# Second attention on one Trainium2 core: explicit job tables, the last maxima turned one batch on, and two small bank reads moved from VectorE to ScalarE

## What is computed

```python
mixed_q, mixed_k, mixed_v = h @ wq + bq, h @ wk + bk, h @ wv + bv
glo = jnp.mean(mixed_q, axis=1, keepdims=True)
c = jnp.tanh(mixed_q @ wfq + bfq + (glo @ wfg + bfg))
p, z = jnp.sum(heads(c) * up, -1), jnp.sum(heads(c) * uz, -1)
P, Z = sigmoid(p) * S, sigmoid(z) * S
G = -(j - P[..., None]) ** 2 * 2.0 / Z[..., None] ** 2
probs = softmax(q @ k.T / sqrt(8) + G)
x = layernorm(h + (probs @ v) @ wo + bo)
```

## Time and profile before

| what | value |
|---|---|
| median of 3 runs | 1585.86 us (1583.54 to 1586.01) |
| the profiled execution | 1584.24 us |
| its span | 1582.5 us |
| mean granted clock of PE | 0.966 |
| PE busy | 1426.4 us, 90% of the span |
| DVE busy | 1126.6 us, 71% |
| ACT busy | 989.4 us, 63% |
| POOL busy | 832.0 us, 53% |

### The profile page before, as it was taken

The page is one execution under the profiler, slowest core; times in us unless marked ns, Lnnn a source line. Parts: engine busy times, 40 slices in busy tenths (PEclk is TensorE's granted clock), DMA queues, the critical chain, the costliest instruction groups (busy, mean ns, idle before and its releaser), DMA issues. The chain is left out here.

```text
span 1582.5 us, 37924 instructions
## 1 busy us (share of the span) xinstructions
PE 1426.4 (90%) x12249; PEld 809.1 (51%) x12249; DVE 1126.6 (71%) x2583; ACT 989.4 (63%) x2120; POOL 832.0 (53%) x1008
## 2 busy tenths in 40 slices
PE   5999999999999999999979999888888888887837
PEld 4666666666666666666646776522332332332225
DVE  5657666666767657666677888878888888888733
ACT  2656656656666666666647888647677677665711
POOL 4766776776776776776665545511231231232533
PEclk9999999999999999999979999979999999999969
DMA  6100000100000000000000000241111111111000
GB/s 193 30 22 23 27 21 20 27 20 20 27 20 20 27 20 20 25 22 20 21 17 1 0 0 21 60 116 49 34 33 50 30 37 47 30 45 31 14 24 17
DMA packets 71099, 50.82 MB, mean 32 GB/s; under 512 B 30875, under 2 KB 59408, under 8 KB 70896
## 3 DMA queue, kind: packets, MB, share of 16 engines
q1 hardware_dynamic: 67936, 45.70, 10.6%
q10 hardware_dynamic: 1760, 3.02, 0.6%
q0 software_dynamic: 1344, 1.33, 0.3%
HBM read 38.18 MB, written 13.28 MB: 33 GB/s over the span
## 5 line engine op out<-in xcount | busy, mean ns | idle before, releaser
L620 ACT ACTIVATE prob<-score_ps,nmax 128x512 f32<-128x512 f32 (+3 forms) x512 | 266.8, 528 | 148.6 <-DVE nmax L691 148.6
L691 DVE TENSOR_REDUCE nmax<-score_ps 128x1 f32<-128x512 f32 (+3 forms) x512 | 224.9, 480 | 184.9 <-PE score_ps L498 180.0
L1974 DVE TENSOR_REDUCE a_nm<-a_s 128x1 f16<-128x512 f32 x512 | 323.7, 685 | 44.3 <-PE a_s L1810 41.6
L1932 ACT ACTIVATE a_pt<-a_st 128x1024 f32<-128x1024 f32 x256 | 261.8, 1024 | 120.8 <-PE a_st L1814 119.7
L1810 PE MATMUL a_s<-a_kop,a_qop 64*128 64x512 f16 x512 | 184.4, 403 | 61.9 <-DVE a_nm L1974 54.7
L510 PE MATMUL pt_ps<-ident,prob 128*128 128x128 f32 x1280 | 182.7, 273 | 2.6 <-ACT pt L629 1.4
L629 ACT ACTIVATE pt<-pt_ps 128x512 f32<-128x512 f32 (+1 forms) x192 | 102.9, 536 | 123.8 <-PE pt_ps L510 123.8
L1814 PE MATMUL a_st<-a_qop,a_kop 64*128 64x512 f16 x512 | 175.0, 394 | 0.0
L1846 PE MATMUL a_pv<-a_pt,a_vaug 128*32 128x256 f32 x2048 | 167.3, 399 | 7.6 <-ACT a_pvs L1937 6.1
L814 POOL TENSOR_SCALAR_AFFINE_SELECT k_h<-k 64x512 f16<-64x512 f32 x130 | 81.0, 623 | 169.9 <-ACT k L653 157.4
L510 PEld LDWEIGHTS pt_ps<-ident,prob 128*128 128x128 f32 x1280 | 145.6, 141 | 35.2 <-ACT pt L629 1.6
(11 more groups left out here) (386 smaller groups left out, 3130.8 us busy)
## 6 DMA issues: line engine op xcount, KB each, us to landing
r_bc<-r_parts SPq DMA_DIRECT2D x128, 128.0 KB, 2.8
a_qop<-q_parts SPq DMA_DIRECT2D x64, 64.0 KB, 1.9
a_kop<-k_parts SPq DMA_DIRECT2D x64, 64.0 KB, 1.9
x_tok<-in_L_attn_input_dram SPq DMA_DIRECT2D x4, 512.0 KB, 12.8
r_parts<-rsum SPq DMA_DIRECT2D x128, 2.0 KB, 2.1
q_parts<-a_q_h SPq DMA_DIRECT2D x16, 128.0 KB, 2.3
k_parts<-a_k_h SPq DMA_DIRECT2D x16, 128.0 KB, 2.3
e_w<-in_L_ffn_w_dram SPq DMA_DIRECT2D x1, 2048.0 KB, 9.6
```

Of the source, the lines that this page charges most:

```text
L620: ins = nc.scalar.activation(prob[h][:, P_OFF[c]:P_OFF[c] + w], score_ps[u][:, col:col + w], ACT.Exp, bias=nmax[h][:, c:c + 1], accum_out= ...
L691: ins = nc.vector.tensor_reduce(nmax[h][:, c:c + 1], score_ps[u][:, col:col + P * (c + 1)], AX.X, ALU.max, negate=True)
L1932: nc.scalar.activation(pt[kc % 2][r][:, :, :], st_ps[r][:, :, :], ACT.Exp, scale=1.0 / SC).then_inc(exp_done[r], 1)
L1974: nc.vector.tensor_reduce(nm[g % 2][:, c, hh:hh + 1], s_ps[j][:, :], AX.X, ALU.max, negate=True).then_inc(max_done[j], 1)
```

## The change

The two tables become one table for each kind of batch, by half slot. In a middle batch the same twenty jobs run. nm3 moves from half slot 31 to half slot 0 of the next batch, ctx1 from 1 to 30 of the batch before; behind every job with a part on DVE stands a half slot without a job. GB comes before K. The bank reads of V and of GB move from DVE to ACT. In the prelude K and GB change places.

```diff
-        AHEAD = {1: "XT", 2: "Q", 3: "K", 4: "GB", 5: "F", 6: "PZ", 11: "CF", 12: "V"}
+        AHEAD = {1: "XT", 2: "Q", 3: "GB", 4: "K", 5: "F", 6: "PZ", 11: "CF", 12: "V"}
...
-PREP = ["XT", "Q", "K", "GB", "F", "PZ", "CF", "V"]
-MIDDLE = {4: "nm0", 8: "nm1", 9: "CT", 10: "OUT", 12: "nm2", 13: "RX", 15: "RD"}
-END = {0: "ctx1", 1: "XT", 2: "Q", 3: "RC", 4: "ctx2", 5: "K", 6: "GB", 7: "F", 8: "ctx3", 9: "PZ", 11: "CF", 12: "ctx0",
-       13: "V", 14: "RL", 15: "nm3"}
+PREP = ["XT", "Q", "GB", "K", "F", "PZ", "CF", "V"]
+JOBS = {
+    "first": {1: "XT", 3: "Q", 4: "GB", 5: "K", 8: "nm0", 9: "F", 11: "PZ", 16: "nm1", 21: "CF", 22: "ctx0", 24: "nm2", 29: "V",
+              30: "ctx1"},
+    "middle": {0: "nm3", 1: "XT", 3: "Q", 4: "GB", 5: "K", 6: "ctx2", 8: "nm0", 9: "F", 11: "PZ", 14: "ctx3", 16: "nm1", 17: "CT",
+               19: "OUT", 21: "CF", 22: "ctx0", 24: "nm2", 25: "RX", 27: "RL", 29: "V", 30: "ctx1"},
+    "last": {0: "nm3", 5: "RC", 6: "ctx2", 8: "nm0", 14: "ctx3", 16: "nm1", 17: "CT", 19: "OUT", 22: "ctx0", 24: "nm2", 25: "RX",
+             27: "RL", 30: "ctx1"},
+    "tail": {0: "nm3", 6: "ctx2", 7: "RC", 14: "ctx3", 16: "CT", 18: "OUT", 26: "RX", 29: "RL", 30: "RD"},
+}
...
-BEHIND = ["ctx1", "ctx2", "ctx3", "CT", "OUT", "RX", "RL"]
-PARTS_OF = {"first": ("ahead", "own"), "middle": ("ahead", "own", "behind"), "last": ("own", "behind", "RC"),
-            "tail": ("behind", "RC", "RD")}
+BEHIND = ["nm3", "ctx2", "ctx3", "CT", "OUT", "RX", "RL"]
...
 def uses(kind):
-    order = [t[at] for at in range(SLOTS) for t in (MIDDLE, END) if at in t]
-    return [u for u in order if part_of(u) in PARTS_OF[kind]]
+    return [JOBS[kind][h] for h in sorted(JOBS[kind])]
...
     def act_steps(act):
...
+        def gate_bias(kind, b, nb):
+            used(kind, b, "GB")
+            nc.scalar.activation(gbias[:, :], misc[:, 0:1], ACT.Identity, bias=bf[:, :], scale=1.0 / S).then_inc(misc_out, 1)
+
+        def values(kind, b, nb):
+            act.wait_ge(vaug_done, G * nb)
+            used(kind, b, "V")
+            nc.scalar.activation(v32[:, :], misc[:, :], ACT.Copy).then_inc(misc_out, 1)
...
     def dve_steps(dve):
...
-        def values(kind, b, nb):
-            dve.wait_ge(vaug_done, G * nb)
-            used(kind, b, "V")
-            nc.vector.tensor_copy(v32[:, :], misc[:, :]).then_inc(misc_out, 1)
-
-        def gate_bias(kind, b, nb):
-            used(kind, b, "GB")
-            nc.vector.scalar_tensor_tensor(gbias[:, :], misc[:, 0:1], 1.0 / S, bf[:, :], ALU.mult, ALU.add).then_inc(misc_out, 1)
...
-                    for half, table in ((0, MIDDLE), (1, END)):
+                    for half in range(2):
...
-                        if at in table:
-                            shared_use(table[at], kind, b)
+                        job = JOBS[kind].get(2 * at + half)
+                        if job:
+                            shared_use(job, kind, b)
...
-            def maxima_t(kind, b, _, g):
+            def maxima_t(kind, b, cb, g):
                 for k in range(2):
-                    pe.wait_ge(max_done[k], 32 * b + 8 * g + 8)
+                    pe.wait_ge(max_done[k], 32 * cb + 8 * g + 8)
...
-            def maxima(kind, b, _, g):
+            def maxima(kind, b, cb, g):
 
-                act.wait_ge(nm_in[(g + 2) % G], NM_LOADS * (b + 1) if g >= 2 else NM_LOADS * b)
+                act.wait_ge(nm_in[(g + 2) % G], NM_LOADS * (cb + 1) if g >= 2 else NM_LOADS * cb)
```

More of the change, by code:

```diff
@@ L1513, in coefficients @@
             nc.scalar.activation(coef_t[:, :], misc16[:, 0:S], ACT.Copy).then_inc(misc_out, 1)
-        return used, high, {"XT": high("XT", xt_h, xt_hi), "Q": queries, "K": keys, "F": gates, "PZ": sigmoids,
-                            "CF": coefficients}
+        return used, high, {"XT": high("XT", xt_h, xt_hi), "Q": queries, "K": keys, "GB": gate_bias, "F": gates, "PZ": sigmoids,
+                            "CF": coefficients, "V": values}
     def dve_steps(dve):
@@ L1545, in centres @@
             nc.vector.tensor_scalar(cent[:, :, :], cent[:, :, :], S / 32.0, -(S - 1) / 64, ALU.mult, ALU.add).then_inc(cent_done, 1)
-        return used, low, {"XT": low("XT", xt_h, xt_l, xt_hi), "V": values, "GB": gate_bias, "PZ": centres}
+        return used, low, {"XT": low("XT", xt_h, xt_l, xt_hi), "PZ": centres}
     def pool_steps_(pool):
@@ L1718, in shared_use @@
             def shared_use(name, kind, b):
[L1719 to L1725, removed]
+                batch = {"ahead": b + 1, "behind": b - 1}.get(part_of(name), b)
+                if name[-1] in "0123":
+                    step(name[:-1], kind, b, batch, int(name[-1]))
+                else:
+                    step(name, kind, b, batch)
             def batch(kind, b):
```

## The result

The changed kernel takes 1594.11 us (median of 4 runs, 1592.94 to 1594.53), the kernel before beside it 1585.34: a ratio of 1.0056, 95% interval 1.0038 to 1.0073. Five further runs later gave 1593.30 against 1586.27, 1.0043 [1.0029, 1.0057]. So the change costs 7 to 9 us. The profiled execution took 1593.99 us with a span of 1592.3, which is 9.8 more than before.

The account below looks back on a forecast made before the run. No engine is full, so waits between engines bound the kernel. Middle batches +12.2, first batch -.7 and last batch -.5 give +11 us on the profiled 1584.24, 1595.2, and with the runs' median 1596 us; range 1580 to 1603.

Parts of the forecast that it names:

- main case: Whole kernel: jobs standing alone show their whole latency, so the change is slower, 1592 to 1598 us; chance .50.
- Spreading and its savings in the middle batches: Six middle batches: new half slots sum to 59.77 against 57.7 us, 2.0 more each, 12.2 in all.
- the rules' 57.7: Old middle batch followed half by half with timing rules read from the timelines: 57.7 us against the measured 58.0.
- bound from below: Middle batch: at in-a-row costs, CT, PZ, OUT and RX give back .3 + .9 + .8 + .5; some 57.3 us.
- nm3: Halves 31 and 0: moved one batch on, they take 2.97 instead of 3.76 us, a gain of .8.
- The reads on ACT: V and gate bias halves: DVE's .60 and .31 us leave its path, covered by slack between ACT's exponentials.
- The clock: Rival: all six middle batches run at a mean clock of 0.97, +3.2 us, 1599; chance .15.
- The first batch: First batch: gains on V and a hidden Q, loses on ctx1, gives away nm3; -.7 us.
- The last batch: Last batch: ctx2's transposes under RC gain 2.4 us, ctx3, CT, RX and ctx1 alone cost 1.9; -.5.
- Tail and prelude: Tail: nm3 later but T of half 0 sooner, 0 within 1 us; prelude: 0 within .5.
- no more alone: Rival: jobs cost no more alone, DVE waits before PZ, OUT, CT, RX stay, only savings remain: 1572 us; chance .20.
- The rival of a late row of nm3: Rival: nm3's row is late for half 4, PE waits .5 to 1 us per batch, up to 1602; chance .05.

Follow-up runs that it names:

- e1: The kernel before, with PZ moved from half slot 19 to 20 and OUT from 20 to 22: 1601.38 us, ratio 1.0104.
- e3: The kernel before, with V's and the gate bias's bank reads moved from DVE to ACT and nothing else: 1582.69 us, ratio .9983.
- e4: The changed kernel with another table, keeping ctx3, CT, PZ, OUT, V in a row at half slots 17 to 21: 1558.71 us, .9831 against the kernel before.
- e12: The table of e4, with the shift, exponentials and choice of the seventh batch's routing one slot later in the tail: 1556.28 us, .9809 against the kernel before.

## Why the prediction was right, and which steps were wrong

The forecast was 1596.0 and the time 1594.1, slower by .56%, inside the main case's 1592 to 1598. The mechanism is shown: the same DVE waits appear where they were put, one pair of moved jobs in the old kernel costs 1.73 a batch, and putting one job back takes it away. That the total is 1.2 us from the 1595.2 worked out for the profiled execution is luck in part. Against the sum, the middle batches cost 1.1 more (two errors that cancel: 4.3 less from the places, 5.5 more from the clock), the last batch 2.3 more, the first 2.5 less, and the start and what follows the last batch 2.1 less.

- *Spreading and its savings in the middle batches* were put at 12.2 us (2.0 a batch) and measured 7.9 (1.31 at full clock). By quarters the new table came out at 14.2, 14.6, 16.8 and 13.8 against 14.3, 14.7, 17.0 and 13.8, so the new side was good to .4. PZ measured 3.42 (3.44), OUT 3.85 (3.90), CT 2.68 (2.65), XT 2.61 (2.65), RX 3.04 (2.96), V 2.23 (2.25). The transposed maxima took 1.66, not 1.77, three times in a batch. The other .3 came from the base: the new table's sum was set against the rules' 57.7 instead of the measured 58.02, although the text knew of the gap. In its bound from below, CT's .3 does not follow from its own halves either, 2.65 against 2.50.
- *Inside that sum*, nm3 was put at .8 a batch. In the old table it gave 1.1 to 1.2, since ctx1 behind it also got quicker; in the new one, where ctx1 stands elsewhere, halves 31 and 0 take 1.20 + 1.66 instead of 3.76, so .9. The reads on ACT were put at .9 (.60 and .31). They gave .45 in the old table, all of it V's, and .1 in the new one; that step failed: the gate bias half takes the same either way, and in the new table ctx1's transposes stand right behind ACT's copy of V. The sum does not suffer, since its halves for V, GB and ctx1 (2.25, 1.45, 1.90) were measured at 2.23, 1.42 and 1.88; only what they were put down to is wrong. ACT's bias step took .262, not .2, and in the middle batches no one waited for it, as predicted. By VectorE: DVE Perf Modes in the Trainium skill (the errata section's table) it was estimated at .14; the row differs, and the row decides.
- *The clock* was a rival with a chance of .15 and 3.2 us, and nothing for it stood in the sum. It gave 5.5 us beside the main case, not in place of it: there were two stretches of half clock in three of the middle batches and one in a fourth, while the rival counted one in each, at .8 instead of about 1. The step that failed is treating it as another case: the stretches start right behind PZ's and OUT's halves, the ones that the main case makes longer. The rival's reading that PE stands still for more than 2 us there is also wrong: the matmuls' longest idle time is 1.54 us in the old middle batches (the row of 1236.61 below) and 1.58 in the new ones, behind OUT, and .96 behind PZ alone.
- *The first batch* was put at -.7 and gave -3.2, of which 2.0 are the new places. The prediction priced four of its halves and not the others. It took the prices from full-clock batches, while this batch ran at 0.71; whether that matters was not tried. The start moved by -1.3, which is no effect of the change: with the same work ahead of it, it was 1018.1 in one run and 1019.9 in two others.
- *The last batch* was put at -.5 (2.4 gained by RC ahead of ctx2, 1.9 lost by jobs alone) and gave +1.8. The second term was near: half slots 11 to 31 took 38.4 instead of 36.4, and the old ones had a stretch of half clock there (at 1475.1, some .5 us), so about 2.5. The first failed: RC's place is worth .2 (25.6 against 25.8), or .3 by the run with RC later. It counted the wait taken away from ctx2 and not the .75 that RC itself waits when PE comes to it late, nor the .59 that its prefix copy loses beside POOL.
- *Tail and prelude*, put at 0 within 1, gave -.8 in what follows the last batch.

Of the signs named ahead, the waits before PZ, OUT and RX, V's .60 and the missing wait before ctx2 were there. At the loop's end PE no longer waits for the last maximum (the transposes of the maxima waited nine times before, 6.4 us in all, and once now, .2). "With no one waiting" for ACT's copy of V was not there: PE's weight load for ctx1 stood .4 us behind it in each of six batches, and ctx1's half is 1.88 instead of the 1.69 that it takes with the copy on DVE. DVE's idle time rose by 2.1 us a batch where 2.6 was expected, from 9.5 and not from the 10.9 of the prediction, which its own row (58.0 long, 48.5 busy) does not give. The rival "no more alone" (1572) was wrong at the point named for it, the waits before PZ, OUT, CT and RX; its number is nearly what the old row of jobs gives with nm3 and the reads alone (1574.1). The rival of a late row of nm3 did not come: no PE wait for it in the middle batches.

## What to carry to other kernels

A job that passes through three engines costs its whole latency each time the engine at its end has caught up; right behind another such job that engine is late, and the latency is hidden. So price a slot by what stands in the slot before, put the long jobs in a row behind one another, and read the idle time in front of the last engine's step. Compare a sum by rules only with a sum by the same rules or with the measured one, not the two mixed, and count a clock that falls on the same stalls on top of the main case.

## What the runs showed of the hardware

**The stretches of half clock start behind PE's longest idle times.** The profiles here have 53 of them in middle batches. All but one start within 2.8 us after the end of OUT's half slot (0.5 to 2.8) or, where PZ stands alone, 0.9 to 1.5 us after the end of its own. The other one, in e1, starts inside PZ's half. With the reads on ACT in the old table (e3) one began every 58.0 us in six batches (1119.6, 1177.6, 1235.7, 1293.7, 1351.7, 1409.7).

They also go with how long PE's matmuls stand still behind OUT's: 1.54 or 1.58 us in eleven profiles, which have 52 of the stretches in 66 batches. In the old table with PZ and OUT apart (e1), where both halves are about as long as in the change, it is 1.25, and one stretch came in six batches. In the table of rows (e4, e12), where V's matmuls stand right behind OUT's, it is .76, and none came in twelve. PE's idle time in the whole batch does not order them: 9.6 us in e1, 6.9 in e3. The row behind OUT in e1, then in e4:

```profile
1244.07 0.39 PE L1810 MATMUL a_s<-a_kop,a_qop 64*128 64x512 f16 x1 [1.25 <-DVE a_nm L1974]
```

```profile
1222.82 0.39 PE L1809 MATMUL a_s<-a_kop,a_qop 64*128 64x512 f16 x1 [0.76 <-DVE a_nm L1973]
```

But the idle time alone does not decide. These two rows are from one profile of the kernel before, at the same place of the batch. The first stands 1.2 us ahead of a stretch of half clock, the second in a batch that had none:

```profile
1118.95 0.39 PE L1810 MATMUL a_s<-a_kop,a_qop 64*128 64x512 f16 x1 [1.54 <-DVE a_nm L1974]
...
1236.61 0.39 PE L1810 MATMUL a_s<-a_kop,a_qop 64*128 64x512 f16 x1 [1.54 <-DVE a_nm L1974]
```

What decides between the two stays open. It also varies from run to run: the change had seven in the middle batches of one run and six in another.

**DVE held up by POOL.** Two kinds of DVE step that read only SBUF take longer when POOL's addition of 128x512 runs beside them, and then end .05 to .12 us after it. In e4 a subtraction on 128x32 elements took 1.79 us, ending at 1465.34 where POOL's addition ended at 1465.29; in the change RC's prefix copy took .83, ending at 1451.04 where POOL's ended at 1450.92. Over all profiles the copy took .80 to 1.00 in the eight where the addition ran beside it and .24 or .25 in the six where it did not. The subtraction took .38 to 1.79 in the seven with the addition and .19 elsewhere. The Trainium skill (SBUF — State Buffer, the section on who interferes with whom) says that some of DVE's instructions and GpSimd's share a pair of ports that one of them holds to its end. These rows agree with that, with one open point: in e4 DVE's row starts .45 us ahead of POOL's addition, at 1463.55 against 1464.00. No run here took POOL's step away alone.

**Chips differ in the last batch.** Where the kernel before took 1602.79, the last batch took 77 to 80 us in all four variants profiled there, against 61 to 65 elsewhere, with DVE waits of this kind in the old kernel with nm3 moved:

```profile
1467.38 0.26 DVE L1980 RECIPROCAL a_rsum<-a_misc 128x16 f32<-128x16 f32 x1 [6.54 <-remote]
```

The middle batches there were as elsewhere. That is four profiles on one chip; the kernel before was not profiled there, and the cause was not tried. Ratios from that chip are therefore of kernels with a longer common part.
